# Head of a two-layer graph kernel: order of the loads of x, order of its products, and ACT's loads and squares

## The reference

```
sim = jnp.tanh(adj * simlar)              # simlar is adj here
filt = sim * (adj > 0)
new_adj = top_k(filt, 350), scattered back
h2 = jnp.tanh(x @ W_proj + b_proj)
feat = relu(new_adj @ (h2 @ W_gcn) + b_gcn)
x = layernorm(x + feat)
pos, neg = (adj > 0) @ x, (adj < 0) @ x
y = concat(pos, neg) @ node_w + node_b * diag + (adj @ x) @ edge_w + edge_b * diag
x = layernorm(x + y)
```

## Time and profile before

| | us |
|---|---|
| median of 3 runs | 618.94 |
| lowest, highest | 618.13, 620.25 |
| the profiled execution | 618.95 |
| its span in the trace | 617.2 |
| TensorE busy in it | 603.0 |
| VectorE, ScalarE, GpSimd busy | 472.7, 417.5, 186.9 |

### The profile page before, as it was taken

How to read it: one execution, slowest core, us unless ns; L and a number is a source line. 1 busy time by engine, 2 the same in 40 slices (tenths; PEclk the granted TensorE clock), 3 DMA queues, 4 the chain that set the end, 5 groups by cost and what they waited for, 6 DMA issues and landing times.

```text
span 617.2 us, 5685 instructions
## 1 busy us (share of the span) xinstructions
PE 603.0 (98%) x1970; PEld 344.5 (56%) x1970; DVE 472.7 (77%) x683; ACT 417.5 (68%) x297; POOL 186.9 (30%) x80
## 2 busy tenths in 40 slices
PE   7799999999999999999999999999999999999995
PEld 6644444444444444555555655655655656558994
DVE  2577879797887879986787697796787786887733
ACT  3387686868686786648884783883893884865850
POOL 0387796978879796200000000000000000000000
PEclk9799999999999999999999999999999999999998
DMA  8999999999999990047898399387486685783000
GB/s 236 336 343 343 336 281 314 273 327 276 323 292 309 291 236 1 1 137 193 234 248 241 107 252 254 100 244 220 135 252 174 172 243 147 210 242 110 2 17 19
DMA packets 141181, 130.65 MB, mean 212 GB/s; under 512 B 9443, under 2 KB 141158, under 8 KB 141158
## 3 DMA queue, kind: packets, MB, share of 16 engines
q1 hardware_dynamic: 74982, 66.22, 38.9%
q10 hardware_dynamic: 66176, 64.17, 37.4%
HBM read 128.27 MB, written 2.10 MB: 211 GB/s over the span
## 4 chain that ended last, share of the span: by engine, by line
PE 95%; DMA 2%; ACTq 1%; ACT 1%; DVE 0%; issue 0%; DVEq 0%
PE acc L939 36%; PE acc L953 33%; PE stage L962 10%; PE stage L961 10%; PE stage L953 2%; DMA x_rows<-in_x_dram 2%; PE to_rows L968 1%; PE to_rows L967 1%; ACTq L462 1%; PE stage L907 1%; PE to_rows L924 1%; ACT a_cols L525 0%; PE to_cols L913 0%; PE stage L902 0%; ACTq L465 0%
## 5 line engine op out<-in xcount | busy, mean ns | idle before, releaser
L592 DVE STREAM_TRANSPOSE a_cols<-a_rows 128x2048 f32<-128x2048 f32 x128 | 294.5, 2306 | 87.8 <-PE stage L962 53.0
L939 PE MATMUL acc<-a_cols,rhs 128*128 128x512 f32 x512 | 221.1, 592 | 0.7 <-ACT a_cols L525 0.7
L953 PE MATMUL acc<-a_cols,x_rows 128*128 128x512 f32 (+1 forms) x512 | 216.2, 565 | 0.0
L359 POOL TENSOR_TENSOR a_cols<-a_cols 128x1536 f32<-128x1536 f32 x64 | 175.3, 2749 | 63.7 <-DVE a_cols L592 62.7
L939 PEld LDWEIGHTS acc<-a_cols,rhs 128*128 128x128 f32 x512 | 96.7, 190 | 119.4 <-issue 119.4
L525 ACT ACTIVATE a_cols<-a_cols 128x2048 f32<-128x2048 f32 x64 | 122.4, 1912 | 53.4 <-POOL a_cols L359 52.3
L953 PEld LDWEIGHTS acc<-a_cols,x_rows 128*128 128x128 f32 x512 | 96.0, 189 | 86.3 <-issue 81.0
L541 ACT ACTIVATE a_rows<-a_rows 128x4096 f32<-128x4096 f32 x32 | 116.0, 3624 | 25.6 <-DVE a_cols L592 12.6
L961 PE MATMUL stage<-masks,x_hi 128*128 128x512 f32 (+1 forms) x288 | 126.8, 449 | 0.0
L544 ACT ACTIVATE a_rows<-a_rows 128x4096 f32<-128x4096 f32 x32 | 116.0, 3623 | 1.0
L962 PE MATMUL stage<-masks,x_lo 128*128 128x512 f32 (+1 forms) x288 | 103.1, 367 | 0.0
(11 more groups left out here) (103 smaller groups left out, 238.9 us busy)
## 6 DMA issues: line engine op xcount, KB each, us to landing
a_rows<-in_adj_dram SPq DMA_DIRECT2D x120, 512.0 KB, 9.0
a_rows<-in_adj_dram ACTq DMA_DIRECT2D x120, 512.0 KB, 10.1
out_dram<-n_rows SPq DMA_DIRECT2D x28, 64.0 KB, 8.5
x_rows<-in_x_dram SPq DMA_DIRECT2D x6, 128.0 KB, 4.1
x_rows<-in_x_dram ACTq DMA_DIRECT2D x6, 128.0 KB, 5.4
x_rows<-in_x_dram SPq DMA_DIRECT2D x4, 64.0 KB, 2.1
x_rows<-in_x_dram ACTq DMA_DIRECT2D x4, 64.0 KB, 2.4
diag<-in_adj_dram SPq DMA_DIRECT2D x16, 1.0 KB
```

Of the source, the lines that this page charges most:

```text
L359: nc.gpsimd.tensor_tensor(part, part, part, ALU.mult).then_inc(squared_pool, 1)
L592: nc.vector.transpose(half_out(hs), half_in(s, h % HALVES)).then_inc(turned[layer], 1)
L939: last = nc.tensor.matmul(acc[parity][:], rhs[:, b, :], a_cols[:, h % HSLOTS, k, :], start=(b == 0), stop=(b == BLOCKS - 1))
L953: last = nc.tensor.matmul(sums, x_rows[:, b, :], rows(a_cols[:, h % HSLOTS, k, :]), start=(b == 0), stop=(b == BLOCKS - 1))
```

## The change

Five things are changed, all in the head and in the first chunk of layer 0.

- Loads of x: SP issues part 1 ahead of W_proj and b_proj. ACT issues parts 1 and 2 ahead of W_gcn, and b_gcn behind x's last part, with a semaphore of its own, for which ACT waits only behind the head.
- Order of the uses: rhs 4 now stands ahead of turn 6, rhs 5 between turns 6 and 7, and turn 7 ahead of hid 6. Ahead of turn 6, TensorE does 8 products of the tile of ones (128 columns each) into the bank that turn 6 writes, and waits for x's last part only then. The order becomes

```diff
--- before.py
+++ after.py
@@ -66,7 +66,9 @@
     X_PARTS = [4, 4, 8, 8, 8]
     X_FIRST = 4
     WARM_UP = 7
-    EARLY = [("turn", 7), ("rhs", 4), ("rhs", 6)]
+    ACT_FIRST = 3
+    KEEP_WARM = 8
+    EARLY = [("rhs", 4), ("rhs", 5), ("rhs", 7)]
 
     ctx = ExitStack()
     with ctx:
@@ -218,6 +220,7 @@
         x_loaded = [sem(f"x_loaded{k}") for k in range(len(X_PARTS))]
         proj_loaded = sem("proj_loaded")
         gcn_loaded = sem("gcn_loaded")
+        b_gcn_loaded = sem("b_gcn_loaded")
         wl1_loaded = sem("wl1_loaded")
         a_loaded = [sem(f"a_loaded{k}") for k in range(SLOTS)]
         zeroed = sem("zeroed")
@@ -298,12 +301,17 @@
 
 
         GROUPS = BLOCKS // TILES
+        X_LAST = sum(X_PARTS[:X_FIRST]) // TILES
         turns, hids, rhss = ([(kind, g) for g in range(GROUPS)] for kind in ("turn", "hid", "rhs"))
         USES = turns[:2]
-        for k in range(GROUPS):
-            USES += hids[k:k + 1] + rhss[max(k - 2, 0):max(k - 1, 0)] + turns[k + 2:k + 3]
-        USES += rhss[GROUPS - 2:]
-        by_dve = [k == "turn" or (k == "rhs" and g not in (1, 3)) for k, g in USES]
+        for k in range(X_LAST):
+            USES += hids[k:k + 1] + rhss[max(k - 2, 0):max(k - 1, 0)] + turns[:X_LAST][k + 2:k + 3]
+
+        USES += rhss[X_LAST - 2:X_LAST - 1] + turns[X_LAST:X_LAST + 1] + rhss[X_LAST - 1:X_LAST] + turns[X_LAST + 1:]
+        for k in range(X_LAST, GROUPS):
+            USES += hids[k:k + 1] + rhss[k - 1:k] * (k > X_LAST)
+        USES += rhss[GROUPS - 1:]
+        by_dve = [(k == "turn" and g < GROUPS - 1) or (k == "rhs" and g not in (1, 2, 3)) for k, g in USES]
         HEAD = [stage[0][:], stage[1][:], stage[2][:], stage[3][:], to_cols[:],
                 to_rows[:].rearrange("p t f -> p (t f)")]
 
@@ -375,9 +383,10 @@
                         .then_inc(a_loaded[s], 16)
 
             load_x(0)
+            load_x(1)
             sp.dma_start(w_pg[:, 0, :], w_proj).then_inc(proj_loaded, 16)
             sp.dma_start(b_col[:, 0:1], b_proj.rearrange("(p a) -> p a", a=1)).then_inc(proj_loaded, 16)
-            for part in range(1, X_FIRST):
+            for part in range(2, X_FIRST):
                 load_x(part)
             load_piece((0, 0), 0)
             for part in range(X_FIRST, len(X_PARTS)):
@@ -471,15 +480,30 @@
             load_x(0)
             act.wait_ge(consts, 1)
             nc.scalar.activation(signs[:, 0:1], ones[:, 0:1], ACT.Tanh)
+            load_x(1)
+            load_x(2)
             act.dma_start(w_pg[:, 1, :], w_gcn).then_inc(gcn_loaded, 16)
-            act.dma_start(b_col[:, 1:2], b_gcn.rearrange("(p a) -> p a", a=1)).then_inc(gcn_loaded, 16)
-            for part in range(1, X_FIRST):
+            for part in range(3, X_FIRST):
                 load_x(part)
             load_piece((0, 0), 0)
             for part in range(X_FIRST, len(X_PARTS)):
                 load_x(part)
 
+            act.dma_start(b_col[:, 1:2], b_gcn.rearrange("(p a) -> p a", a=1)).then_inc(b_gcn_loaded, 16)
+
             act.wait_ge(proj_loaded, 32)
+
+            waiting = iter([(rows_of(0, chunk), s, q) for chunk in ((0, 0, 0), (1, 0, 1)) for s in range(PIECES)
+                            for q in ACT_QUARTERS][len(ACT_QUARTERS):])
+
+            def load_next():
+                load_quarter(*next(waiting))
+
+            def square_rest(n):
+                rest = flat(a_cols, n % HSLOTS)[:, SQ_POOL:]
+                act.wait_ge(turned[0], n + 1)
+                nc.scalar.activation(rest, rest, ACT.Square).then_inc(squared_act, 1)
+
             for n, (kind, g) in enumerate(USES):
                 if by_dve[n]:
                     continue
@@ -487,13 +511,18 @@
                 if kind == "hid":
                     nc.scalar.activation(group(h_t, g), bank_of(n), ACT.Tanh, bias=b_col[:, 0:1])\
                         .then_inc(stage_act, 1)
-                    if g >= 2:
-                        load_quarter((0, 0), g // 2, ACT_QUARTERS[g % 2])
+
+                    if g >= ACT_FIRST:
+                        load_next()
+                    if g == 6:
+                        square_rest(0)
+                elif kind == "turn":
+                    nc.scalar.copy(group(feat_t, g), bank_of(n)).then_inc(stage_act, 1)
                 else:
                     nc.scalar.copy(rhs[:, g * TILES:(g + 1) * TILES, :],
                                    bank_of(n).rearrange("p (b f) -> p b f", f=F)).then_inc(stage_act, 1)
 
-            act.wait_ge(gcn_loaded, 32)
+            act.wait_ge(b_gcn_loaded, 16)
 
             def relu_out(chunk):
                 c, q, parity = chunk
@@ -514,16 +543,20 @@
                     n = c * HPC + h
                     hs = h % HSLOTS
                     act.wait_ge(turned[0], n + 1)
-                    if h % HALVES == HALVES - 1 and chunk is not LAST:
+                    if h % HALVES == HALVES - 1 and before and chunk is not LAST:
                         load_piece(rows_of(0, next_of(chunk)), h // HALVES)
-                    rest = flat(a_cols, hs)[:, SQ_POOL:]
-                    nc.scalar.activation(rest, rest, ACT.Square).then_inc(squared_act, 1)
+                    if h or before:
+                        square_rest(n)
                     if h == 7 and before:
                         high_part(before)
                     act.wait_ge(squared_act, n + 1)
                     act.wait_ge(squared_pool, n + 1)
                     nc.scalar.activation(a_cols[:, hs, :, :], a_cols[:, hs, :, :], ACT.Tanh)\
                         .then_inc(tanh_done, 1)
+                    if not before:
+                        load_next()
+                if not before:
+                    load_next()
 
             each_chunk(layer0)
             relu_out(LAST)
@@ -897,17 +930,21 @@
                     emptied(pe, n - len(HEAD))
                 bank = bank_of(n)
                 if kind == "turn":
+                    if g == X_LAST:
+
+                        for _ in range(KEEP_WARM):
+                            nc.tensor.matmul(bank[:, 0:P], ones[:], ones[:], start=True, stop=True)
                     pe.wait_ge(x_loaded[part_with(g * TILES)], 16 * QUARTERS)
                     for k in range(TILES):
                         last = nc.tensor.transpose(bank[:, k * P:(k + 1) * P], x_rows[:, g * TILES + k, :], ident[:])
                 elif kind == "hid":
                     if g == 0:
                         pe.wait_ge(proj_loaded, 32)
-                    pe.wait_ge(stage_dve, count_of("turn", g))
+                    emptied(pe, USES.index(("turn", g)))
                     last = nc.tensor.matmul(bank, w_pg[:, 0, :], group(feat_t, g), start=True, stop=True)
                 else:
                     if g == 0:
-                        pe.wait_ge(gcn_loaded, 32)
+                        pe.wait_ge(gcn_loaded, 16)
                     pe.wait_ge(stage_act, count_of("hid", g))
                     for k in range(TILES):
                         last = nc.tensor.matmul(bank[:, k * P:(k + 1) * P], blk(h_t, g * TILES + k),
```

## The result

The changed kernel took 616.88 us (median of 22 runs, 615.87 to 620.27) against 619.12 us for the kernel before (22 runs, 617.86 to 620.76). The ratio is 0.9975, with a 95% interval from 0.9965 to 0.9985: faster by 0.25%, some 1.6 us by the ratio and 2.2 us by the medians, where 4.8 us were forecast. The median lies just inside the range that was given (up to 616.9), whose upper end was there for the rivals; the main case, 613.2 to 615.0, was missed, and the size of the effect is a third to a half of the forecast. A second set of 12 runs gave 616.82 us (ratio 0.9957, 0.9936 to 0.9978).

What follows compares the result with a forecast made beforehand. TensorE runs through from its first layer-0 product, whose start sets the end; moving it from 31.8 to 27.0 us takes 4.8 us off 618.95, forecast 614.1 us, range 613.0 to 616.9.

Steps and rivals of the forecast that it cites:

- T0: Start of TensorE's first layer-0 product, the only number forecast: from 31.8 to 27.0 us, 4.8 us earlier.
- the main case: Whole kernel at 613.2 to 615.0 us, without any rival; chance 0.68.
- x's last part: Load of x in the head: lands at 19.8 us, between 19.2 and 20.6, against 20.32 before.
- From turn 6 to T0: End of the head: turn 6 starts at 20.1 us, the first layer-0 product at 27.0.
- x's third part: Load of x (part 2) awaited by TensorE until 9.02 us: 1.2 us earlier, 7.8, ends 7.4 and 9.0.
- From 10.4 the head runs through.: TensorE's head, first to fifth rhs group with turns and hid products: 7.9 us without waits, to 18.3 us.
- Behind a full queue that doesn't move its landing.: Second adjacency piece: issue on ACT moves from 14.07 to about 15.4 us, landing stays at 26.2.
- TensorE never waited for this, so it is worth nothing.: One ACT load per tanh instead of pairs that held its squares: no gain.
- A: Rival: first chunk starves, TensorE waits for half 2 or 4; costs 1 to 2 us, 615.6 us; chance 0.14.
- B: Rival: clock falls all the same, chain behind x's last part at 1.2 GHz; costs 2.5 us, 616.7; chance 0.10.
- C: Rival: products put ahead of x's last part wait for ACT and push turn 6 back; 617.7 us; chance 0.04.
- D: Rival: slower, chunk 1 runs dry because ACT's single loads land late; some 621 us; chance 0.04.

Runs made afterwards that it cites:

- e5: Changed kernel with ACT's adjacency loads starting behind hid tanh 2 instead of 3, none behind the tanh of half 0; 615.24 us, ratio 0.995.
- e1: The changed kernel run again, nothing altered; 616.82 us, ratio 0.9957 to the kernel before.
- e15: The same kernel as e5 run again; 615.99 us, ratio 0.9952 to the kernel before.
- e4: Changed kernel with ACT's adjacency loads of chunks 0 and 1 as before: one per hid tanh from group 2, then pairs; 619.28 us, ratio 0.9992.
- e11: Kernel before with ACT's adjacency loads issued singly, one behind each tanh from hid tanh 2 on; 618.02 us, ratio 0.9975.
- e3: Changed kernel with b_gcn's load issued only after the head's last hid tanh; 617.9 us, ratio 0.998.
- e10: e5 with the square of half 0 back behind the head's last tanh; 616.9 us, ratio 0.9956.
- e6: Changed kernel with x's parts, W_gcn and b_gcn issued in the order of before; 616.64 us, ratio 0.9969.

## Why the prediction was wrong

**The bound was read rightly, and the way to an earlier T0 in the main.** In the kernel before TensorE runs through from T0 on, and T0 was set by x's last part and the clock. The reordered head does what it says: in the changed kernel TensorE does not wait more than 0.65 us for x's last part, its clock stays up, and the chain from the first rhs group to turn 6 took 9.70 us in e5 where the prediction's steps make 9.7. From turn 6 to T0 it put 6.9 us; 6.55 to 6.61 were measured. POOL and DVE were never in the way of half 0. Taking e1, whose profiled execution is at the median, the forecast T0 of 27.0 became 28.86 by 1.0 (first rhs group at 11.39, not 10.4), 1.0 (turn 4 at 13.26, when rhs 0 had ended at 12.28), 0.2 (small gaps) and -0.3 (turn 6 to T0). Behind T0 it lost another 0.7. That is 2.6 us of the 4.8. The next four paragraphs take the steps that failed: two terms ahead of T0, which make most of the 1.9 us there, and one wait behind it.

**x's third part** was taken at 7.8 us, with 9.0 as the other end. It came at 8.4 to 9.0 in the profiles of the new order, 8.69 and 8.64 in the changed kernel's two. The sum had moved it by what ACT's half gains, although SP's half has the same bytes ahead of it as before. By the Trainium skill (DMA: Bandwidth & Descriptors, Queues, rings and completion order) one queue is consumed in order; that would have spoken for the upper end, and the prediction weighed it for the last part alone. The 8.4 to 9.0 us fit it, though they don't show it. This term is 0.8 of the 1.0 us by which the first rhs group was late in e1.

**"From 10.4 the head runs through."** x's fourth part was put at nothing, without a reason. TensorE waited 1.12 and 0.74 us for it at turn 4 in the changed kernel's two profiles, and turn 4 came 1.0 us later than the sum has it. In both, ACT's first tanh was also outside its bounds (10.37 and 10.56, for 9.1 to 10.0), because the issue of x's last part, for which the sum took the time of before, held ACT's queue longer: 3.42 us from 6.17 on, against 2.36 before. What makes the issue and the fourth part late in some executions is not shown. x's last part itself landed at about 23.1 and 22.2 us (its last DMA took 13.5 and 14.5 us) for a forecast of 19.8; in e5, with a busy second queue, at about 20.5.

**"Behind a full queue that doesn't move its landing."** This is the step that failed in mechanism. The prediction saw that ACT's first adjacency load moves by one hid tanh and priced it at nothing, since the queue was full in the kernel before. It did not count how long the queue stays full once nothing is put in: but for b_gcn's half kilobyte, ACT's part of x's last part was issued by 9.6 us, and the next load came at 15.05. In 16 to 22 us ACT's queue moved 0.14, 0.02 and 0.10 MB, against 0.29, 0.31 and 0.35 before: some 0.7 MB less, an estimate of 2 us at the 350 GB/s that both queues move together. The landing did move. The last DMA of the second piece was issued at 14.07 and landed at 26.2 before; in e5 it was issued at 14.08 and landed 12.7 us later, at 26.8; in e1 at 16.98 and 28.2, in the first set's profile at 17.24 and 29.8, where the prediction had it issued at about 15.4 and landed at 26.2. The first piece was late as well, off the path to T0: half 0's transpose began at 20.3 in e1 and at 18.4 in e5, where the prediction had the piece at 18.1. The transpose of half 2, which needs it, in e1 and in e5:

```profile
28.17 2.31 DVE L625 STREAM_TRANSPOSE a_cols<-a_rows 128x2048 f32<-128x2048 f32 x1 [0.34 <-DMA a_rows<-in_adj_dram]
...
26.86 2.31 DVE L625 STREAM_TRANSPOSE a_cols<-a_rows 128x2048 f32<-128x2048 f32 x1
```

With a load at hid tanh 2 the time is 0.8 to 1.6 us lower. Where that lies is seen best in e15, whose T0 (29.64) is nearly that of the first set's profile (29.78) and whose rest is 1.3 us shorter: 1.0 us of that is the wait for the relu and 0.2 us the wait for half 2, both behind T0.

**"TensorE never waited for this, so it is worth nothing."** ACT's single loads were priced from a timeline in which ACT had slack. In the new head the gain hangs on them: 616.0 or 615.2 us with them (e15, e5), 619.3 with pairs (e4), the same loads from the same tanh on. In the old head e11 leaves open whether they were worth something too. As I read it, TensorE's earlier start brings ACT to its loads earlier, the DMAs are no earlier, and the difference is spent in a blocked issue. Of the changed kernel itself the profile shows the remainder of this, at the first place where ACT issues a pair again:

```profile
54.09 5.08 ACTq L474 DMA_DIRECT2D a_rows<-in_adj_dram  x2
59.22 0.63 ACT L505 ACTIVATE a_cols<-a_cols 128x512 f32<-128x512 f32 x1 [3.22 <-issue]
...
61.70 0.67 ACT L530 ACTIVATE z_t<-acc,b_col 128x512 f32<-128x512 f32 x1
```

The first pair takes 5.08 us to issue, the last two single loads in front of it, at 50.10, took 3.22 us; the squares behind them start 1.4 and 3.2 us late, and the relu at 61.70 is what TensorE waits 1.0 us for.

**The rivals.** A, the first chunk starves, had 0.14 and was right in kind: the second piece did land late, by 2.0 and 3.6 us. But TensorE's wait for half 2 was nothing in e1 and 0.24 us in the other profile; it waited for a relu in chunk 1. That A's price, 1 to 2 us, is near what was missing is luck, since most of that lay ahead of T0. B happened in some executions only: of the 22 of the first set the four with a mean granted clock of 0.993 or 0.994 took 618.98 to 620.27 us, the others 615.87 to 619.31. C, with 0.04, came true by its sign in e1 and e5: turn 6 started at 22.25 and 21.39 us without a wait for x, because the work put in front of it began late and the idle products stood there; in e1 x's last part was just as late. D did not happen; it had the right place, ACT's loads of chunk 1, and the wrong direction, since the queue is too full there and not too empty.

## What to carry to other kernels

When an engine issues DMAs between its instructions, both states of its queue had a price here: empty, the other queue did not make up for it (0.35 MB in 2 us with or without it); held up, the engine stood still with all that is behind the issue. So when a start is moved forward, follow each issue to the next one on its queue, and put the issues behind long instructions, never ahead of one that is awaited. In a sum of the kind "start + constant" look at the constant too: here it was 587.2 and 586.1 with the first load behind hid tanh 3 (the changed kernel) and 585.5 and 585.9 with it behind hid tanh 2 (e5, e15). And a part that has moved in its queue is to be priced for each queue that carries a half of it.

## What was not expected of the hardware

- SP's queue all but alone moved no more than when it shared the engines: 0.35 MB in 2 us, some 175 GB/s, at 107.2% of the engines' time, against 0.35 MB at 58.8% beside a busy second queue. e3's profile has the same, 0.37 MB at 106.2% beside 0.02 MB. The packets are of 0.9 KB in the mean; why they take longer is not shown.
- The issue of a DMA can hold its engine for 2.23 us at half a kilobyte and 5.68 us for a pair of 512 KB, and one load of 512 KB took 0.32 us where nothing held it up. So its size does not set it; that a full queue does is inferred from the loads issued before.
- Gaps of nearly the same length at the same place, turn 2, cost the clock in some executions and not in others: 1.24 us (e10) and 1.60 us (e3) did, 1.12 us (e1) and 1.78 us (e6) did not. The Trainium skill (TensorE: Matmul & The Clock Gate, Part 1) says that the transition point is not tied to the kernel's start. These four profiles fit that; they do not prove it.
